# Attention and expert layer on one core: value products in three groups of four slots, and row-maximum units placed anew

## The chip, the cores and the metric

The kernel runs on one core of a Trainium2 chip. The metric is the device time of one execution in microseconds (us); lower is better. TensorE multiplies (PE in the rows; PEld is its weight load), VectorE is DVE, ScalarE is ACT, GpSimd is POOL, and SyncE (SP) issues most DMA transfers. The engines run their own instruction lists in order and meet at semaphores.

## The reference

One transformer layer on 8 batches of 1024 tokens of width 256: causal attention with 16 heads of 64, then a router over 32 experts with a capacity of 320 tokens.

```python
q_blhd = jnp.einsum('bld,dhk->blhk', x_bld, Wq)
latent_bll = jnp.einsum('bld,dc->blc', x_bld, Wkv_down)
k_blhd = jnp.einsum('blc,chk->blhk', latent_bll, Wk_up)
v_blhd = jnp.einsum('blc,chk->blhk', latent_bll, Wv_up)
attn = softmax(where(mask, q @ k / sqrt(64), neg_inf))
y_blhd = jnp.einsum('bhqk,bkhd->bqhd', attn, v_blhd)
x = _layernorm(x + jnp.einsum('bqhd,hdo->bqo', y_blhd, Wout))
x = _layernorm(x + _L0_ffn_ref(x, w_router, w_gate, w_up, w_down))
```

## The kernel before

Key and value projections are folded, so that scores are products of a projected query with a latent of 64 columns, and the value product multiplies probabilities with the latent itself (`lat_keys`). The outer loop runs over 64 **pairs** of heads (`gp`; `b` is the batch and `p` = 0 to 7 the pair in it). Each pair has 12 **slots** `t`: slots 0 to 3 are the first 512 queries against key tiles 0 to 3, slots 4 to 11 the second 512 queries against key tiles 0 to 7. Slots 0 to 3 and 8 to 11 lie on the diagonal and shrink (512, 384, 256, 128 queries); the other four have 512.

For a slot TensorE writes turned scores, keys on partitions, into one of three banks (`turned_scores`, L742 and L745; the two that shrink most hold both heads in one bank); ScalarE takes the exponential into one of NPROBS probability buffers (L1011); GpSimd zeroes the masked half of a diagonal block (`keep_past`, L491) and adds the buffers up (`add_probs`, L511 and L516); TensorE multiplies them with the latent (`values`, L765), the two heads side by side on 64 output columns each. Two slots make a group of value products, six groups in a pair. A buffer is free when its value product and its addition are done.

The softmax needs each query's maximum a pair ahead. 24 **units** for each pair (`row_scores`, L717, two to a place of PLACES) write untransposed scores into three more banks (`row_ps0`, `row_ps1`, half of `turned_ps1`), and VectorE takes a maximum from each (`row_max`, L1175 with a mask, L1179 without). A unit waits until the unit that had its bank three before is reduced. In PLACES, (t, 0) is after the scores of slot t and (t, 1) after what else the slot does. The places of a pair are numbered 0 to 11 below, in order. VectorE combines the maxima (L1183) and TensorE transposes them ("maxT", `turn_max`, L727, 8 columns), twice a pair, in slots 0 and 6.

LATE is a hand-written list of work by slot that shares one bank, `misc_ps`: the query projection of a later pair ("q", L664; ScalarE writes its high halves at L991 and L992, VectorE then its low halves at L1155 and L1156, and only then is the bank free), maxT, the sums ("sums", L777, inverted by VectorE at L1196 and spread by `invert_rows` at L1209 and L1213 in slots 6 and 8), and, in some pairs, the output projection ("proj", L787), transposes of x ("xT") and of its normalised sum ("x1T"), latents ("lat"), keys and the router. "proj" stands in pairs p = 0 and 1 of a batch, x1T in p = 2, xT and lat in p = 6, keys in p = 7. After the 64 pairs come the experts, which the change leaves in their order.

VectorE walks the same list: in a slot first the maxima of the units at (t, 0), then the low halves of a query from slot t-1, then the rest of LATE, `invert_rows`, and the units at (t, 1).

## Time and profile before

| | |
|---|---|
| median of 3 runs | 2441.88 us (2440.73 to 2442.39) |
| the profiled execution's own time | 2441.89 us |
| its span, first to last instruction | 2440.1 us |
| PE busy | 2319.8 us, 95% |
| POOL busy | 1715.3 us, 70% |
| DVE busy | 1517.1 us, 62% |
| ACT busy | 1041.7 us, 43% |
| mean granted TensorE clock | 0.974 |

Busy time is a union over an engine's instructions. TensorE's ends are modelled, so starts are what is read: the distance from one matmul's start to the next is what the first one costs. The three windows of 27.00 us from 147.20 on hold one pair each (p = 3, 4, 5 of batch 0), and repeat to within 0.02 us in TensorE's busy time; they stand for the pairs without extra work.

### The profile page before, as it was taken

The numbers are of one execution on the slowest core, as the hardware profiler recorded it, in microseconds if no ns is written. First come the engines' busy times: TensorE is split into PE (matmuls) and PEld (weight loads), VectorE is DVE, ScalarE is ACT, GpSimd is POOL, SyncE is SP. The second block draws the span as 40 slices with busy tenths as digits, with TensorE's granted clock in tenths as the row PEclk, the third lists the DMA queues.
The fourth block names the chain that finished last, engine by engine and source line by source line (L and its number), as shares of the span: only waits on it lengthen the run. The fifth ranks groups of instructions, "written<-read, shape, count | busy, mean of one in ns | idle before, by whom it ended". The sixth has DMA issues, their size and how long they took to land.

```text
span 2440.1 us, 36843 instructions
## 1 busy us (share of the span) xinstructions
PE 2319.8 (95%) x11528; PEld 1509.0 (62%) x11528; DVE 1517.1 (62%) x4450; ACT 1041.7 (43%) x2048; POOL 1715.3 (70%) x1774
## 2 busy tenths in 40 slices
PE   6999999999999999999999999999999999849996
PEld 5565576556655666567655765566656665537774
DVE  4677656765576657765776567656766577225553
ACT  3454435543455445443544354534554454112222
POOL 0688767986788667975797669867886679524444
PEclk8999999999999999999999999999999999969998
DMA  3222200200011001100020002100110011234552
GB/s 89 62 65 62 62 10 19 65 24 18 14 44 49 14 14 36 53 19 14 19 73 21 10 19 61 27 18 14 44 49 14 14 33 41 67 110 150 183 184 67
DMA packets 96819, 118.97 MB, mean 49 GB/s; under 512 B 12288, under 2 KB 75782, under 8 KB 96624
## 3 DMA queue, kind: packets, MB, share of 16 engines
q1 hardware_dynamic: 89712, 99.98, 14.9%
...
q8 instruction: 93, 1.52, 0.3%
...
## 4 chain that ended last, share of the span: by engine, by line
PE 83%; DVE 7%; issue 4%; POOL 3%; ACT 2%; DMA 0%; SPq 0%; DVEq 0%; POOLq 0%; ACTq 0%
PE value_ps L765 20%; PE misc_ps L787 9%; PE turned_ps L742 9%; PE turned_ps L745 9%; PE misc_ps L664 8%; PE row_ps L717 7%; PE turned_ps L938 6%; PE turned_ps L717 3%; PE misc_ps L777 2%; DVE rinv L1209 1%; PE value_ps L957 1%; PE misc_ps L957 1%; POOL half_sums L516 1%; DVE masked_row L1175 1%; PE misc_ps L813 1%
## 5 line engine op out<-in xcount | busy, mean ns | idle before, releaser
L1011 ACT ACTIVATE probs<-turned_ps 128x512 f32<-128x512 f32 (+2 forms) x1280 | 647.7, 555 | 779.6 <-PE turned_ps L745 749.1
L516 POOL TENSOR_TENSOR half_sums<-half_sums,probs 128x1024 f32<-128x1024 f32 (+3 forms) x512 | 832.2, 1625 | 30.0 <-ACT probs L1011 14.1
L765 PE MATMUL value_ps<-probs,lat_keys 128*64 128x512 f32 (+3 forms) x3072 | 589.1, 505 | 2.2 <-POOL probs L491 2.2
L742 PE MATMUL turned_ps<-q_hl,lat_hi 128*128 128x512 f32 (+2 forms) x1280 | 500.2, 393 | 1.5 <-ACT fold_v L1064 1.5
L745 PE MATMUL turned_ps<-q_max,lat_lo 65*128 65x512 f32 (+2 forms) x1280 | 480.4, 375 | 1.8 <-DMA q_max<-both_rows 1.8
L491 POOL TENSOR_SCALAR_AFFINE_SELECT probs<-probs 128x256 f32<-128x256 f32 x512 | 210.6, 411 | 354.6 <-ACT probs L1011 352.0
L1175 DVE CUSTOM_DVE_ANT_0 masked_row<-row_ps,future 128x512 bf16<-128x512 f32 (+4 forms) x707 | 344.7, 508 | 136.5 <-PE row_ps L717 130.4
L765 PEld LDWEIGHTS value_ps<-probs,lat_keys 128*64 128x64 f32 x3072 | 188.2, 137 | 278.0 <-issue 211.6
L511 POOL TENSOR_TENSOR half_sums<-probs 128x768 f32<-128x768 f32 (+1 forms) x128 | 269.6, 2106 | 118.7 <-ACT probs L1011 118.6
L717 PE MATMUL row_ps<-lat_hi,q_hl 128*128 128x512 f32 (+4 forms) x1026 | 340.6, 373 | 4.9 <-DVE neg_max L1175 4.0
L717 PEld LDWEIGHTS row_ps<-lat_hi,q_hl 128*128 128x128 f32 x1026 | 189.6, 191 | 150.7 <-issue 69.7
L742 PEld LDWEIGHTS turned_ps<-q_hl,lat_hi 128*128 128x128 f32 x1280 | 243.3, 190 | 39.2 <-ACT probs L1011 10.0
L745 PEld LDWEIGHTS turned_ps<-q_max,lat_lo 65*128 65x128 f32 x1280 | 244.2, 191 | 27.7 <-DMA q_max<-both_rows 2.3
L1179 DVE TENSOR_REDUCE unit_max<-row_ps 128x1 f32<-128x512 f32 (+1 forms) x319 | 199.9, 643 | 77.0 <-PE row_ps L717 77.0
L787 PE MATMUL misc_ps<-fold_v,headsT 128*128 128x256 f32 x1008 | 232.5, 383 | 6.3 <-DVE x L1237 3.6
L787 PEld LDWEIGHTS misc_ps<-fold_v,headsT 128*128 128x128 f32 x1008 | 187.6, 190 | 47.4 <-issue 13.9
L717 PE MATMUL turned_ps<-lat_hi,q_hl 128*128 128x320 f32 x510 | 182.4, 358 | 6.5 <-DVE unit_max L1175 2.7
L523 POOL TENSOR_TENSOR headsT<-headsT,rinv_rows 128x512 f32<-128x512 f32 x128 | 165.4, 1292 | 22.7 <-DVE rinv_rows L1213 22.7
L991 ACT CAST q_hl<-misc_ps 64x512 fp32r<-64x512 f32 x125 | 72.6, 581 | 216.6 <-PE misc_ps L664 216.6
L1175 DVE CUSTOM_DVE_ANT_0 masked_row<-turned_ps,future 128x256 bf16<-128x256 f32 (+1 forms) x317 | 160.6, 507 | 3.4 <-PE turned_ps L717 1.5
L938 PE MATMUL turned_ps<-ex_xT,ex_w 128*128 128x320 f32 x512 | 145.6, 438 | 0.0
L1237 DVE TENSOR_TENSOR x<-misc_ps,x_in 128x256 f32<-128x256 f32 x64 | 27.2, 425 | 186.7 <-PE misc_ps L787 186.7
...
## 6 DMA issues: line engine op xcount, KB each, us to landing
q_max<-q_hl SPq DMA_DIRECT2D x256, 128.0 KB
...
```

Of the source, the lines that this page charges most:

```text
L491: nc.gpsimd.affine_select(out=block, in_=block, pattern=[[0, 2], [1, P]], compare_op=ALU.is_ge, fill=0.0, base=0, channel_multiplier=-1).t ...
L511: nc.gpsimd.tensor_tensor(sums_of(gp, c)[:, :, q0:BANK], before[:, :, q0:BANK], now[:, :, q0:BANK], ALU.add).then_inc(added, 1)
L516: nc.gpsimd.tensor_tensor(total, total, now[:, :, q0:BANK], ALU.add).then_inc(added, 1)
L717: nc.tensor.matmul(dst[:, 0:k1 - k0], q_hl[gp % 2][:, h, i * P:(i + 1) * P], lat_hi[b % 2][:, k0:k1], start=True, stop=True).then_inc(rows ...
L742: nc.tensor.matmul(scores_of(n, h), lat_hi[b % 2][:, keys], q_hl[gp % 2][:, heads, cols], start=True, stop=False)
L745: nc.tensor.matmul(scores_of(n, h), lat_lo[b % 2][:, keys], q_max[:, c, heads, q0:BANK], start=False, stop=True).then_inc(turned_full, 1)
L765: mm = nc.tensor.matmul(value_ps[h * LD:(h + 1) * LD, q0:BANK], lat_keys[b % 2][:, j, :], probs[:, n % NPROBS, h, q0:BANK], start=(j == 0) ...
L787: mm = nc.tensor.matmul(bank[:, 0:D], headsT[:, (NPAIR * b + j) % NHEADS, i * P:(i + 1) * P], fold_v[:, j, :], start=(j == 0), stop=(j == ...
L938: mm = nc.tensor.matmul(turned_ps[f][:, m, 0:C], ex_w[e % AHEAD][:, m, kd, f * P:(f + 1) * P], ex_xT[:, g % 2, kd, u * C:(u + 1) * C], sta ...
L1011: nc.scalar.activation(probs[:, n % NPROBS, heads, q0:BANK], scores_of(n, h), ACT.Exp).then_inc(exp_done, 1)
L1175: nc.vector.tensor_tensor_reduce(masked_row[n % 2][:, 0:width], row[:, 0:width], future[:, BANK - width:], scale=-1.0, scalar=-MASKED, op0 ...
L1179: nc.vector.tensor_reduce(dst, row[:, 0:width], AX.X, ALU.max, negate=True).then_inc(max_done, 1)
```

## The change

Value products go in groups of four slots: slots 8 to 11 of the pair before in slot 1, slots 0 to 3 in slot 5, slots 4 to 7 in slot 9, each two slots behind its scores. There are eight probability buffers instead of six. The room comes from x: one buffer instead of two, and x is loaded a second time, straight into `x1`, where the output projection is added to it in place. The 12 places of the units, the sums (slot 4 to 5) and some LATE work (slot 5 to 4) move. `NOUT` only names a 2.

```diff
-    PLACES = [(0, 0), (0, 1), (1, 1), (2, 1), (4, 0), (4, 1), (6, 0), (7, 0), (8, 0), (8, 1), (10, 0), (10, 1)]
+    PLACES = [(0, 0), (1, 0), (1, 1), (3, 1), (4, 1), (5, 0), (5, 1), (7, 0), (8, 1), (9, 0), (9, 1), (10, 1)]
...
-    NPROBS = 6
-    VALUES = 2
+    NPROBS = 8
+    VALUES = 4
...
-        x_in = [sb(f"x_in{i}", [P, NT, D], F32, attn) for i in range(2)]
+        x_in = sb("x_in", [P, NT, D], F32, attn)
...
             if gp:
-                late[4].append(("sums", gp - 1))
+                late[5].append(("sums", gp - 1))
...
-                for i, t in enumerate((3, 5, 9, 10, 11)):
+                for i, t in enumerate((3, 4, 9, 10, 11)):
                     late[t].append(("proj", b - 1, 3 + i))
...
-                                  (3, 5, 7, 10)):
+                                  (3, 4, 7, 10)):
                     late[t].append(("x1T", b - 1, *use))
...
-                for t, c in zip((3, 5, 7, 8), (0, 2, 1, 3)):
+                for t, c in zip((3, 4, 7, 8), (0, 2, 1, 3)):
                     late[t].append(("xT", b + 1, c))
...
-                late[5].append(("keys", b + 1))
+                late[4].append(("keys", b + 1))
...
+                if p == NPAIR - 1:
+                    if b:
+                        sp.wait_ge(sent, 16 * NT * b)
+                    sp.dma_start(x1[:, :, 0:D], x_tiles[b]).then_inc(x1_loaded, 16)
...
-                    if t % VALUES == LAG % VALUES and gp * NSLOT + t >= VALUES + LAG:
-                        values(gp * NSLOT + t - LAG - VALUES)
+                    n0 = gp * NSLOT + t - LAG - (VALUES - 1)
+                    if n0 >= 0 and n0 % VALUES == 0:
+                        values(n0)
...
-                nc.vector.tensor_tensor(x1[:, i, 0:D], bank[:, 0:D], x_in[b % 2][:, i, :], ALU.add).then_inc(free_of(use), 1)
+                nc.vector.tensor_tensor(x1[:, i, 0:D], bank[:, 0:D], x1[:, i, 0:D], ALU.add).then_inc(free_of(use), 1)
```

Place A, TensorE of an ordinary pair before, from the projection "q" of slot 1 (its last row) to the second unit of place 4 (`row_ps0`, 128x320). L717 are units, L742 and L745 turned scores, L765 value products.

```order
L664 MATMUL misc_ps<-xT_lo,fold_hi 128x512 x2
L717 MATMUL row_ps1<-lat_hi0,q_hl1 128x384
L717 MATMUL turned_ps1<-lat_hi0,q_hl1 128x384
...
L765 MATMUL value_ps<-probs,lat_keys0 64x256 x2
L765 MATMUL value_ps<-probs,lat_keys0 64x128 x2
L717 MATMUL row_ps0<-lat_hi0,q_hl1 128x512
L717 MATMUL row_ps1<-lat_hi0,q_hl1 128x512
...
L717 MATMUL turned_ps1<-lat_hi0,q_hl1 128x320
L717 MATMUL row_ps0<-lat_hi0,q_hl1 128x320
```

The same place in the changed kernel, where lines stand 5 or 6 higher (L722 units, L747 and L750 scores, L670 "q"):

```order
L670 MATMUL misc_ps<-xT_lo,fold_hi 128x512 x2
L722 MATMUL row_ps1<-lat_hi0,q_hl1 128x384
L722 MATMUL turned_ps1<-lat_hi0,q_hl1 128x384
L747 MATMUL turned_ps1<-q_hl0,lat_hi0 128x512
...
L747 MATMUL turned_ps0<-q_hl0,lat_hi0 128x256
...
L722 MATMUL row_ps0<-lat_hi0,q_hl1 128x512
L722 MATMUL row_ps1<-lat_hi0,q_hl1 128x512
...
L722 MATMUL turned_ps1<-lat_hi0,q_hl1 128x320
L722 MATMUL row_ps0<-lat_hi0,q_hl1 128x320
```

The value group between the two uses of `row_ps0` is gone (it now stands ahead of "q").

Place B, VectorE between the two halves of the inversion in an ordinary pair. Before:

```order
L1175 ISA masked_row0,unit_max<-turned_ps1,future 128x256
...
L1175 ISA masked_row1,unit_max<-row_ps0,future 128x256
...
L1179 TENSOR_REDUCE unit_max<-row_ps1 128x1
L1179 TENSOR_REDUCE unit_max<-turned_ps1 128x1
L1209 RECIPROCAL rinv<-sums_cols 32x16 x4
L1213 STREAM_TRANSPOSE rinv_rows1<-rinv 128x512
```

And in the changed kernel (its lines 6 higher):

```order
L1181 ISA masked_row0,unit_max<-turned_ps1,future 128x256
...
L1181 ISA masked_row1,unit_max<-row_ps0,future 128x256
...
L1215 RECIPROCAL rinv<-sums_cols 32x16 x4
L1219 STREAM_TRANSPOSE rinv_rows1<-rinv 128x512
L1185 TENSOR_REDUCE unit_max<-row_ps1 128x1
L1185 TENSOR_REDUCE unit_max<-turned_ps1 128x1
```

The two maxima of place 8 now stand behind the second half of the inversion.

Place C, TensorE of the changed kernel from the value group of slot 9 to maxT of slot 0 in the next pair (L770 value products, L732 maxT):

```order
L770 MATMUL value_ps<-probs,lat_keys0 64x512 x8
L722 MATMUL turned_ps1<-lat_hi0,q_hl1 128x512
L722 MATMUL row_ps0<-lat_hi0,q_hl1 128x512
...
L722 MATMUL row_ps1<-lat_hi0,q_hl1 128x512
L722 MATMUL turned_ps1<-lat_hi0,q_hl1 128x512
...
L722 MATMUL row_ps0<-lat_hi0,q_hl0 128x128
L722 MATMUL row_ps1<-lat_hi0,q_hl0 128x128
L732 MATMUL misc_ps<-ident,neg_max1 8x128
```

Before, one place of units instead of two came between the last value group and slot 11, and another value group stood between the 128x128 units and maxT.

## Rows read from the trace of the kernel before

**Rows 1.** The page, part 1: busy time, share and instructions of TensorE.
```profile
PE 2319.8 (95%) x11528; PEld 1509.0 (62%) x11528; DVE 1517.1 (62%) x4450; ACT 1041.7 (43%) x2048; POOL 1715.3 (70%) x1774
```

**Rows 2.** Busy us of each engine in one ordinary pair, clock, DMA, GB/s.
```profile
147.20:174.20 27.00, 26.85 (x136) 16.13 (x137) 19.58 (x59) 13.43 (x28) 22.81 (x22) 1.00 0.24 70
```

**Rows 3.** Timeline of TensorE, that pair: start us, us, engine, line, tile.
```profile
152.08 0.87 PE L765 MATMUL value_ps<-probs,lat_keys 128*64 128x256 f32 x8
152.88 0.50 PE L717 MATMUL row_ps<-lat_hi,q_hl 128*128 128x512 f32 x1
...
161.50 0.27 PE L727 MATMUL misc_ps<-ident,neg_max 128*8 128x128 f32 x1
...
161.84 0.39 PE L745 MATMUL turned_ps<-q_max,lat_lo 65*128 65x512 f32 x1
...
169.59 0.40 PE L717 MATMUL turned_ps<-lat_hi,q_hl 128*128 128x512 f32 x1
169.83 0.40 PE L717 MATMUL row_ps<-lat_hi,q_hl 128*128 128x512 f32 x1
170.16 1.94 PE L765 MATMUL value_ps<-probs,lat_keys 128*64 128x512 f32 x8
172.03 0.50 PE L717 MATMUL row_ps<-lat_hi,q_hl 128*128 128x512 f32 x1
172.36 0.39 PE L717 MATMUL turned_ps<-lat_hi,q_hl 128*128 128x512 f32 x1
```

**Rows 4.** Timeline, all engines, from the end of slot 1's "q".
```profile
151.17 0.34 PE L717 MATMUL row_ps<-lat_hi,q_hl 128*128 128x384 f32 x1
...
153.32 0.69 DVE L1156 TENSOR_TENSOR q_hl<-misc_ps,q_hl 64x512 fp32r<-64x512 f32 x1
...
154.04 0.69 DVE L1175 CUSTOM_DVE_ANT_0 masked_row<-row_ps,future 128x512 bf16<-128x512 f32 x1
...
154.66 0.08 DVE L1175 DVE_READ_ACCUMULATOR2_ANT neg_max<- 128x1 f32 x1
...
154.79 0.19 PEld L717 LDWEIGHTS row_ps<-lat_hi,q_hl 128*128 128x128 f32 x1 [0.19 <-DVE neg_max L1175]
```

**Rows 5.** Timeline from the inversion on VectorE, and TensorE's stop at 163.73.
```profile
157.79 0.41 PE L717 MATMUL row_ps<-lat_hi,q_hl 128*128 128x320 f32 x1
...
157.93 0.72 DVE L1196 STREAM_TRANSPOSE sums_cols<-misc_ps 128x512 f32<-128x512 f32 x1 [1.77 <-PE misc_ps L777]
...
160.58 1.29 DVE L1179 TENSOR_REDUCE unit_max<-row_ps 128x1 f32<-128x512 f32 x2 [1.13 <-PE row_ps L717]
161.88 0.28 DVE L1190 CAST both_rows<-misc_ps 8x128 fp32r<-8x128 f32 x1
...
163.81 0.39 DVE L1175 CUSTOM_DVE_ANT_0 masked_row<-turned_ps,future 128x256 bf16<-128x256 f32 x1
...
164.48 0.69 DVE L1179 TENSOR_REDUCE unit_max<-row_ps 128x1 f32<-128x512 f32 x1
...
163.73 0.39 PE L717 MATMUL row_ps<-lat_hi,q_hl 128*128 128x512 f32 x1
164.27 0.50 PE L717 MATMUL turned_ps<-lat_hi,q_hl 128*128 128x512 f32 x1
```

**Rows 6.** Timeline of VectorE, last units of the pair and the combination.
```profile
172.56 0.69 DVE L1175 CUSTOM_DVE_ANT_0 masked_row<-row_ps,future 128x512 bf16<-128x512 f32 x1 [0.33 <-PE row_ps L717]
...
173.18 0.69 DVE L1175 CUSTOM_DVE_ANT_0 masked_row<-turned_ps,future 128x512 bf16<-128x512 f32 x1
...
173.91 0.17 DVE L1183 TENSOR_REDUCE neg_max<-unit_max 128x8 f32<-128x16 f32 x1
```

**Rows 7.** Timeline of TensorE in a pair p = 6: xT of slot 3, and "q" of slot 9.
```profile
1011.64 0.34 PE L717 MATMUL row_ps<-lat_hi,q_hl 128*128 128x384 f32 x1
...
1014.54 0.66 PE L674 MATMUL misc_ps<-ident,x_in 128*128 128x128 f32 x4 [0.20 <-DVE q_hl L1156]
...
1030.39 0.70 PE L664 MATMUL misc_ps<-xT_hi,fold_hi 128*128 128x512 f32 x2 [0.45 <-DVE xT_lo L1132]
```

More of the change, by code:

```diff
@@ L201, in build_layer @@
         end_free = [sem(f"end_free{i}") for i in range(3)]
-        x_loaded = [sem(f"x_loaded{i}") for i in range(2)]
+        x_loaded = sem("x_loaded")
+        x1_loaded = sem("x1_loaded")
         wkv_split = sem("wkv_split")
@@ L407, in _ @@
                     sp.wait_ge(alone_ready, b)
-                    sp.dma_start(out_tiles[b - 1], x_in[(b - 1) % 2][:, :, :]).then_inc(alone_stored, 16)
-                if b and p == 5 and b + 1 < B:
-                    sp.wait_ge(alone_stored, 16 * b)
-                    sp.dma_start(x_in[(b + 1) % 2][:, :, :], x_tiles[b + 1]).then_inc(x_loaded[(b + 1) % 2], 16)
+                    sp.dma_start(out_tiles[b - 1], x_in[:, :, :]).then_inc(alone_stored, 16)
+                if p == 5 and b + 1 < B:
+                    if b:
+                        sp.wait_ge(alone_stored, 16 * b)
+                    sp.dma_start(x_in[:, :, :], x_tiles[b + 1]).then_inc(x_loaded, 16)
             def load_weights(e):
@@ L432, in _ @@
             sp.wait_ge(alone_ready, B)
-            sp.dma_start(out_tiles[LAST], x_in[LAST % 2][:, :, :]).then_inc(alone_stored, 16)
+            sp.dma_start(out_tiles[LAST], x_in[:, :, :]).then_inc(alone_stored, 16)
             sp.wait_ge(sent, 16 * NT * B)
@@ L447, in _ @@
                 g = (e - AHEAD) // 2
-                sp.wait_ge(ex_sent[g % 2], 16 * NY * (g // 2 + 1))
+                sp.wait_ge(ex_sent[g % NOUT], 16 * NY * (g // NOUT + 1))
                 load_rows(e)
                 load_weights(e)
-            for k in range(2):
-                sp.wait_ge(ex_sent[k], 16 * NY * (E // 4))
+            for k in range(NOUT):
+                sp.wait_ge(ex_sent[k], 16 * NY * (E // 2 // NOUT))
         @block.gpsimd
@@ L671, in turn_x @@
                 kd, t0 = c // 2, HPB * (c % 2)
-                pe.wait_ge(x_loaded[b % 2], 16 * (b // 2 + 1))
+                pe.wait_ge(x_loaded, 16 * (b + 1))
                 for k in range(HPB):
-                    mm = nc.tensor.transpose(bank[:, k * P:(k + 1) * P], x_in[b % 2][:, t0 + k, kd * P:(kd + 1) * P],
-                                             ident[:, :])
+                    mm = nc.tensor.transpose(bank[:, k * P:(k + 1) * P], x_in[:, t0 + k, kd * P:(kd + 1) * P], ident[:, :])
                 mm.then_inc(full_of(use), 1)
@@ L902, in _ @@
                         row_scores(*unit)
-            for n0 in range(PAIRS * NSLOT - VALUES - LAG, PAIRS * NSLOT, VALUES):
-                values(n0)
+            values(PAIRS * NSLOT - VALUES)
             for use in ENDING:
@@ L1029, in pass_alone @@
             def pass_alone(b, i):
+                x_out = x_in
                 act.wait_ge(x1_ready, b * 2 + i // HPB + 1)
                 act.wait_ge(alone_scale, b * 2 + i // HPB + 1)
-                ins = nc.scalar.activation(x_in[b % 2][:, i, :], x1[:, i, 0:D], ACT.Identity, scale=alone[:, 2, i:i + 1])
+                ins = nc.scalar.activation(x_out[:, i, :], x1[:, i, 0:D], ACT.Identity, scale=alone[:, 2, i:i + 1])
                 if i == NT - 1:
```

24 lines of the change are left out of this document (11 added, 13 removed).

## The prediction

> **What bounds the kernel now.** I read the page first: TensorE is busy for 95% of the span, no other engine for more than 70% [rows 1]. Then windows of one pair: of 27.00 us in an ordinary pair TensorE is busy for 26.85 at a granted clock of 1.00 (the 2.4 GHz level), GpSimd for 22.81, VectorE for 19.58, ScalarE for 13.43 [rows 2]. So while the pairs run, what a matmul costs from its start to the next one's start is what counts, and the others matter only where TensorE stops for them. The timeline shows two kinds of loss, which busy time hides.
>
> The first is the change between value products and the rest. Ordinary neighbours of 512 columns start 0.24 us apart (169.59 to 169.83). From the last of them to the value group it is 0.33, and after the group, between 172.03 and 172.36, again 0.33 [rows 3]: 0.09 going in, 0.10 coming out. Inside, a group with 1024 columns for each head takes 170.16 to 172.03, 1.87 us, and one with 384 columns takes 152.08 to 152.88, 0.80. The line through both has 1.07 / 640 = 1.67 ns a column and 0.16 us that don't depend on columns. A group of value products thus costs about **0.35 us** beside its columns, whatever its length.
>
> The second is waits for a unit's bank. There are three banks, so TensorE can be only three units ahead of VectorE's maxima. Place A (slots 1 to 4): "q" ends and the first unit of place 2 starts at 151.17; VectorE then takes that place's maxima and the two low halves (second one at 153.32), starts the first maximum of place 3 at 154.04, and has it at 154.66 + 0.08. TensorE loads for the second unit of place 4, which needs this bank, at 154.79 [rows 4]. That is 3.62 us after "q", and it was waited for by only 0.11. Place B: the second unit of place 8 started 0.54 after the first, 163.73 to 164.27, 0.30 more than ordinary [rows 5]. With some 0.1 behind it and 0.1 for an exponential in slot 5, estimates from the same timeline, an ordinary pair has some 0.6 us of waits.
>
> **What the change saves.** Six groups become three: 3 x 0.35 = 1.05 us a pair. The columns stay.
>
> **What moving maxT costs.** Both maxT (8 columns of weights) stood behind a value group: there maxT and the first score after it take 161.50 to 161.84, 0.34 [rows 3], where without maxT the first matmul takes 0.33. It was free. Now both stand alone. At least 0.10 each (only the first score after it is longer), at most 0.35 each (a full change). I take 0.2, nearer to the entry and exit of 0.19 that the value group shows without its 0.16 inside.
>
> Of this the page "TensorEngine Tiling (Array Packing)" of the Trainium skill, section Key Properties, says that changing the tiling mode drains TensorE. By this rule a maxT alone is a change of its own, and only one of three changes a pair is really saved, 0.35 instead of 0.65 net. The trace agrees for value groups (the 0.35 above) and doesn't show a maxT alone at full clock.
>
> **What the new order costs.** VectorE's list is nearly the same as before (the order shows it), with the same times per instruction. So I walk TensorE against it, from three moments at which VectorE is idle or its place is known. Units and scores cost 0.235 us per 512 columns (0.175 for 384, 0.15 for 320, 0.12 for 256), "q" six times 512, 1.40.
>
> *Place A.* From the end of "q": units 0.35, scores of slots 2 and 3 0.71, place 3 0.47, scores of slot 4 0.94, first unit of place 4 0.15: TensorE is at its second unit after 2.62. It needs the bank of the first unit of place 3, and VectorE's chain to there is unchanged, 3.62 [rows 4]. Before, the value group of 0.80 and its 0.19 stood in between. Wait: **1.00**.
>
> *Place B.* From the first unit of place 6, right behind the sums. VectorE starts the inversion 0.14 later (157.93 against 157.79, where TensorE's next matmul starts) and goes on: inversion 0.72 (less an overlap of some 0.08), maxima of place 6 1.30 (160.58 to 161.88), the maxT copy and the first half of `invert_rows` 1.93 (to 163.81), place 7 0.67 (to 164.48) [rows 5], the second half of `invert_rows` 1.75 (as the first, without the copy), first maximum of place 8 0.69: 7.1, release 7.2. TensorE: place 6 0.57, slot 6 0.94, maxT 0.15, slot 7 0.94, place 7 0.24, slot 8 0.94 with 0.11 of waiting for an exponential, "q" 1.40, place 8 0.47, slot 9 0.70, first unit of place 9 0.18: 6.64. The second unit of place 9 needs that bank. Wait **0.6**, and the 0.11. The maxT here is hidden in it.
>
> *Place C.* From the first unit of place 10, behind the value group of slot 9. VectorE starts 0.53 later (172.03 to 172.56 before), two maxima 1.29, then two masked ones and the combination, 172.56 to 173.91 + 0.17, 1.52 [rows 5, 6]: 3.34. TensorE: place 10 0.57, slot 10 0.47, place 11 0.47, slot 11 0.24, slot 0 0.94, place 0 0.12: 2.81, then maxT, which waits for the combination. A value group used to cover this. Wait: **0.53**, and the 0.2 of maxT behind it.
>
> Ordinary pair: -1.05 + 0.2 + 1.00 + 0.71 + 0.53 - 0.6 = **+0.8 us**.
>
> The other pairs, by the same walk:
> - p = 0: "q" is in slot 7, and its low halves stand ahead of the second half of `invert_rows`. "q" ends 4.24 after the sums; low halves from 1.45 after it, 1.42 for both [rows 4]; 1.75; 0.69: 9.55 against 6.53. Wait 3.0 at place 9 instead of 0.6. The projections of slots 9 to 11 cover place C. -1.05 + 0.2 + 1.00 + 3.06 - 0.2 = +3.0.
> - p = 1: the same at B, and at slot 3 "proj" needs `misc_ps`, free 2.90 after "q" ended (1011.64 to 1014.54, and there TensorE came early, by 0.20 in idle time and some 0.35 in starts [rows 7]). Now it comes at 1.06: wait 1.84 instead of A's 1.00, with 0.35 of waits before. +3.7.
> - p = 2: 1.84 at x1T of slot 3, then x1T cover B and C. +0.3.
> - p = 6: 1.84 at xT of slot 3, and two xT each wait for ScalarE's and VectorE's halves of the one before: 2.75 at A for 0.35, 3.9 at B (xT of slots 7 and 8 ahead of `invert_rows`) for 0.6 (one of 0.45 + 0.15 shown at 1030.39 [rows 7]), 1.0 more at C, where the value group no longer stands ahead of "lat". +5.9. This is the roughest one.
> - p = 7: the copy of the keys comes ahead of place 4. +1.1.
>
> Sum: 27 ordinary pairs 22, p = 0 seven times 21, p = 1 26, p = 2 2, p = 6 seven times 41, p = 7 8: **+120 us** on the profiled execution's 2441.89, which is the median of the runs (2441.88) too. 2562, said as **2560**.
>
> **Costed at nothing.** Second load of x (8 x 1 MB): issued on SP in p = 7 ahead of the next query's transfers, which SP issues after slot 3 and TensorE needs a third of a pair later; `add_x` comes nine slots after. Should it delay that query row by its transfer, each batch pays at most a few us. Waiting for `sent` there stops SP with only that behind it; sending ends a pair earlier. Reading x in place of `x_in` is the same addition. The eight buffers end ScalarE's waits for old value products; TensorE waited for ScalarE by 0.1 a pair. GpSimd: the addition of slot 5 waits for the sums, which read its buffer, now later; from there its 14.3 us to the last diagonal block (22.81 [rows 2] less what lies behind) end 2 us before the value group of slot 1 needs it. The experts are unchanged.
>
> **Rivals.**
> - *The saving decides.* If VectorE gives back those banks early enough, the pair loses 1.05 and pays 0.2: -0.85 x 64 = -54, **2388**. For it: VectorE is idle for 27% of the pair [rows 2]. Against it: at the three places its chain is without idle time in the rows. It decides as soon as the three waits together stay under 1.45 (0.85 + the old 0.6); I have 2.24. Chance 0.12.
> - *Only the ordinary waits.* +0.8 in all pairs, the extra waits of p = 0, 1, 6 lying in each other's shadow: +51, **2493**. Against: each starts from a place where VectorE had caught up. Chance 0.2.
> - *GpSimd too.* In p = 5 and 6 it also sends four tiles, and the value group of slot 5 needs slot 3's mask with 1.3 us to spare. If that is used up, 2 to 3 us in 14 pairs: +35, **2595**. Chance 0.1.
> - *maxT as a full change*, by its upper bound of 0.35 (the section cited above would have it so): +0.15 on most pairs, **2570**. Chance 0.05.
> - *No change of cost*, groups of four paying inside what two groups paid and the waits as long as before: **2442**. Chance 0.03.
>
> **How the numbers follow.** My forecast holds 0.5, by itself 2530 to 2590. To leave out no more than 2 in 10, the range takes in the second and third rival: 2480 to 2600. About 0.2% (5 us) is what a measurement of this kernel can tell from no change. Faster 0.12, same 0.03, slower 0.85.
>
> **What the profile after would show.** Ordinary pairs of 27.8 us instead of 27.0; value groups 192 instead of 384, sixteen records each, with 0.16 + 1.67 ns a column. TensorE idle or late at the second unit of place 4 (3.6 after "q"), the second of place 9, and at maxT of slot 0, all released by VectorE; pairs p = 0, 1 and 6 longer by 3 to 6 us; the stretch of the experts as long as before. I am wrong if ordinary pairs come out under 27.0, which means one of the three chains is shorter than in the rows of before, or if the lost time lies with GpSimd or with the transfer of x.

## The result, and the profile after

The changed kernel takes **2656.42 us** (median of 4 runs, 2655.98 to 2657.02), before 2441.31 us beside it. The ratio is 1.088 (95% interval 1.086 to 1.090): 215 us slower, where the prediction said 120, and 56 us beyond the end of its range. The profiled execution's span is 2655.3 us.

Part 1 of the page of the changed kernel, and the first line of part 4, the chain that ended last:

```profile
PE 2392.5 (90%) x11528; PEld 1573.3 (59%) x11528; DVE 1501.8 (57%) x4450; ACT 1026.0 (39%) x2048; POOL 1713.8 (65%) x1774
...
PE 68%; DVE 18%; issue 9%; ACT 3%; POOL 1%; DMA 0%; DVEq 0%; SPq 0%; POOLq 0%; ACTq 0%
```

Of VectorE the page of before had 7% in that chain; it is 18% now. And TensorE is *busy for longer* than in [rows 1], 2392.5 us against 2319.8, with the same 11528 matmuls and fewer group changes. That can't be a wait. The mean granted clock points to the reason: 0.946 against 0.974. The trace has only two values of it, 1.00 and 0.50, so that is 2 x 0.054 x 2655 = 287 us at half clock (1.2 GHz) against 2 x 0.026 x 2440 = 127 before.

Windows of one pair each in the changed kernel: an ordinary one (p = 3 of batch 0), then p = 1, 2, 3 and 6 of batch 2. Columns: start and end, us, busy us of TensorE, its weight load, VectorE, ScalarE, GpSimd, granted clock, DMA share, GB/s.

```profile
148.47:176.52 28.05, 26.99 (x136) 16.45 (x135) 19.33 (x59) 13.10 (x27) 22.79 (x22) 1.00 0.24 67
636.06:687.33 51.27, 46.88 (x216) 33.49 (x215) 23.19 (x73) 14.78 (x30) 26.09 (x29) 0.93 0.05 11
687.33:723.25 35.92, 33.07 (x184) 23.10 (x183) 20.93 (x66) 17.67 (x36) 26.10 (x29) 0.95 0.07 16
723.25:755.71 32.46, 30.79 (x145) 18.30 (x144) 22.93 (x67) 16.75 (x35) 19.92 (x19) 0.89 0.04 9
811.64:856.88 45.24, 36.44 (x164) 23.06 (x163) 23.12 (x66) 17.45 (x35) 30.09 (x28) 0.89 0.12 30
```

The last four in the kernel before, in the same order:

```profile
585.77:629.99 44.22, 44.02 (x216) 31.50 (x215) 23.58 (x73) 15.08 (x30) 26.15 (x29) 1.00 0.06 13
629.99:664.15 34.16, 33.57 (x183) 22.72 (x182) 21.55 (x67) 17.74 (x35) 26.11 (x29) 0.96 0.08 17
664.15:693.55 29.40, 29.38 (x145) 17.30 (x145) 22.58 (x66) 16.78 (x36) 20.00 (x19) 0.94 0.04 10
747.52:782.50 34.98, 32.19 (x166) 20.44 (x164) 22.88 (x66) 17.57 (x34) 31.05 (x30) 1.00 0.15 39
```

The ordinary pair is 28.05 us at full clock, 27.8 predicted. Four of the other pairs run in part at half clock. Over batches 1 to 6 this is 6.8 us of each p = 1, 3.4 of p = 2, 6.8 of p = 3 and 10.2 of p = 6. Before, it was 0.7 us of p = 2, 2.7 of p = 3 and none of the others. VectorE's work in a pair grew by 0.35 us at most.

TensorE's timeline in the ordinary pair: maxT of slot 0, place A, maxT of slot 6, place B, the value group of slot 9.

```profile
148.65 0.34 PE L722 MATMUL row_ps<-lat_hi,q_hl 128*128 128x128 f32 x2
149.38 0.27 PE L732 MATMUL misc_ps<-ident,neg_max 128*8 128x128 f32 x1 [0.39 <-DVE neg_max L1189]
...
154.32 0.34 PE L722 MATMUL row_ps<-lat_hi,q_hl 128*128 128x384 f32 x1
...
157.22 0.42 PE L722 MATMUL turned_ps<-lat_hi,q_hl 128*128 128x320 f32 x1
157.95 0.41 PE L722 MATMUL row_ps<-lat_hi,q_hl 128*128 128x320 f32 x1 [0.31 <-DVE neg_max L1181]
...
164.33 0.27 PE L732 MATMUL misc_ps<-ident,neg_max 128*8 128x128 f32 x1
164.36 0.48 PE L747 MATMUL turned_ps<-q_hl,lat_hi 128*128 128x512 f32 x1
164.68 0.40 PE L750 MATMUL turned_ps<-q_max,lat_lo 65*128 65x512 f32 x1
...
169.38 0.33 PE L722 MATMUL row_ps<-lat_hi,q_hl 128*128 128x384 f32 x1
169.94 0.45 PE L722 MATMUL row_ps<-lat_hi,q_hl 128*128 128x384 f32 x1 [0.23 <-DVE unit_max L1185]
170.31 3.65 PE L770 MATMUL value_ps<-probs,lat_keys 128*64 128x512 f32 x16
173.90 0.50 PE L722 MATMUL turned_ps<-lat_hi,q_hl 128*128 128x512 f32 x1
```

All three places wait for VectorE. The second unit of place 4 starts 3.63 us after "q" ended (157.95 - 154.32; predicted 3.62, against [rows 4]). The value group takes 3.59 (predicted 0.16 + 2048 x 1.67 ns = 3.58). A maxT alone at full clock costs 0.03 (164.33 to 164.36) and lengthens the score behind it from 0.24 to 0.32: 0.11, about the predicted lower bound of 0.10.

Two of the new long waits, in p = 1 of batch 2: "proj" of slot 3, and the second unit of place 9.

```profile
644.26 0.48 PE L792 MATMUL misc_ps<-fold_v,headsT 128*128 128x256 f32 x1 [1.68 <-DVE q_hl L1162]
...
665.95 0.34 PE L722 MATMUL row_ps<-lat_hi,q_hl 128*128 128x384 f32 x1
668.87 0.69 PE L722 MATMUL row_ps<-lat_hi,q_hl 128*128 128x384 f32 x1 [2.59 <-DVE unit_max L1185]
```

And short windows there, for each of the two the wait and what follows it:

```profile
641.30:644.70 3.40, 1.72 (x9) 1.36 (x9) 2.42 (x6) 2.53 (x5) 1.27 (x2) 1.00 0.26 58
644.80:648.10 3.30, 3.30 (x9) 2.64 (x8) 0.00 (x0) 0.00 (x0) 3.12 (x4) 0.50 0.07 17
665.90:668.60 2.70, 0.38 (x3) 0.06 (x1) 2.51 (x7) 1.39 (x4) 2.21 (x8) 1.00 0.00 0
668.70:672.00 3.30, 3.13 (x7) 1.06 (x9) 1.67 (x6) 0.00 (x0) 3.30 (x3) 0.50 0.00 0
```

TensorE stood for 1.68 us and for 2.59 us; "proj" behind the first and the value products behind the second ran at a granted clock of 0.50.

In p = 3 it is different. Its 6.8 us at half clock start at 723.3 us, 0.9 us behind the logits of the router, 32 matmuls of 32 columns. TensorE had not stood there: it was busy for 6.09 of the 6.20 us up to 723.2. The logits and the window at half clock, in the changed kernel and then in the kernel before:

```profile
718.82 3.76 PE L818 MATMUL misc_ps<-wr,x1T 128*128 128x32 f32 x32
723.30:730.10 6.80, 6.35 (x21) 3.53 (x21) 4.04 (x15) 2.50 (x5) 3.34 (x5) 0.50 0.01 3
...
658.43 4.60 PE L813 MATMUL misc_ps<-wr,x1T 128*128 128x32 f32 x32
661.20:667.90 6.70, 6.70 (x23) 4.20 (x22) 3.47 (x11) 1.59 (x3) 3.07 (x4) 0.50 0.01 2
```

Half clock at this spot is not new. Before, it comes inside or right behind the logits in six of seven batches, mostly for half as long; in the changed kernel it comes in all seven.

### The profile page after: what moved, and what is told of

Its sections match the earlier page's. It is cut to its first block, busy times and chain, and to the rows that moved or that the text cites. A ratio compares the mean times of both kernels' runs of the same rounds, so it can differ in the third digit from the quotient of the medians.

```text
span 2655.3 us, 36721 instructions
## 1 busy us (share of the span) xinstructions
PE 2392.5 (90%) x11528; PEld 1573.3 (59%) x11528; DVE 1501.8 (57%) x4450; ACT 1026.0 (39%) x2048; POOL 1713.8 (65%) x1774
## 4 chain that ended last, share of the span: by engine, by line
PE 68%; DVE 18%; issue 9%; ACT 3%; POOL 1%; DMA 0%; DVEq 0%; SPq 0%; POOLq 0%; ACTq 0%
PE value_ps L770 21%; PE misc_ps L792 9%; PE misc_ps L670 7%; PE row_ps L722 6%; PE turned_ps L943 5%; PE turned_ps L747 4%; DVE unit_max L1185 4%; PE turned_ps L750 4%; DVE masked_row L1181 4%; DVE rinv L1215 3%; PE misc_ps L782 2%; PE turned_ps L722 2%; DVE q_hl L1162 2%; DVE q_hl L1161 1%; PE misc_ps L962 1%
## 5 line engine op out<-in xcount | busy, mean ns | idle before, releaser
L770 PE MATMUL value_ps<-probs,lat_keys 128*64 128x512 f32 (+3 forms) x3072 | 569.0, 514 | 0.0
L747 PE MATMUL turned_ps<-q_hl,lat_hi 128*128 128x512 f32 (+2 forms) x1280 | 512.0, 401 | 7.7 <-ACT probs L1016 3.2
L750 PE MATMUL turned_ps<-q_max,lat_lo 65*128 65x512 f32 (+2 forms) x1280 | 485.7, 382 | 0.9 <-DMA q_max<-both_rows 0.9
L722 PE MATMUL row_ps<-lat_hi,q_hl 128*128 128x512 f32 (+4 forms) x1026 | 352.7, 376 | 77.6 <-DVE unit_max L1185 60.9
L770 PEld LDWEIGHTS value_ps<-probs,lat_keys 128*64 128x64 f32 x3072 | 211.1, 142 | 305.4 <-issue 274.7
L747 PEld LDWEIGHTS turned_ps<-q_hl,lat_hi 128*128 128x128 f32 x1280 | 249.1, 195 | 94.9 <-ACT probs L1016 52.7
L722 PEld LDWEIGHTS row_ps<-lat_hi,q_hl 128*128 128x128 f32 x1026 | 191.2, 196 | 182.6 <-DVE unit_max L1185 79.2
L750 PEld LDWEIGHTS turned_ps<-q_max,lat_lo 65*128 65x128 f32 x1280 | 248.9, 194 | 31.6 <-DMA q_max<-both_rows 1.6
L792 PE MATMUL misc_ps<-fold_v,headsT 128*128 128x256 f32 x1008 | 244.3, 397 | 15.4 <-DVE q_hl L1162 11.7
L792 PEld LDWEIGHTS misc_ps<-fold_v,headsT 128*128 128x128 f32 x1008 | 195.9, 198 | 61.6 <-DVE q_hl L1162 13.2
L722 PE MATMUL turned_ps<-lat_hi,q_hl 128*128 128x320 f32 x510 | 194.2, 381 | 8.2 <-DVE unit_max L1185 4.8
L1185 DVE TENSOR_REDUCE unit_max<-turned_ps 128x1 f32<-128x512 f32 (+1 forms) x193 | 119.0, 617 | 128.5 <-PE turned_ps L722 113.8
L1241 DVE TENSOR_TENSOR x<-misc_ps,x 128x256 f32<-128x256 f32 x64 | 27.2, 425 | 253.2 <-PE misc_ps L792 253.2
```

The costliest lines, as they stand in the source:

```text
L722: nc.tensor.matmul(dst[:, 0:k1 - k0], q_hl[gp % 2][:, h, i * P:(i + 1) * P], lat_hi[b % 2][:, k0:k1], start=True, stop=True).then_inc(rows ...
L747: nc.tensor.matmul(scores_of(n, h), lat_hi[b % 2][:, keys], q_hl[gp % 2][:, heads, cols], start=True, stop=False)
L750: nc.tensor.matmul(scores_of(n, h), lat_lo[b % 2][:, keys], q_max[:, c, heads, q0:BANK], start=False, stop=True).then_inc(turned_full, 1)
L770: mm = nc.tensor.matmul(value_ps[h * LD:(h + 1) * LD, q0:BANK], lat_keys[b % 2][:, j, :], probs[:, n % NPROBS, h, q0:BANK], start=(j == 0) ...
L792: mm = nc.tensor.matmul(bank[:, 0:D], headsT[:, (NPAIR * b + j) % NHEADS, i * P:(i + 1) * P], fold_v[:, j, :], start=(j == 0), stop=(j == ...
L1185: nc.vector.tensor_reduce(dst, row[:, 0:width], AX.X, ALU.max, negate=True).then_inc(max_done, 1)
```

## The experiments

The theory after the result: the value groups that were taken out had covered waits for VectorE's chain, as predicted, and some of the longer new waits bring TensorE's clock to 1.2 GHz, which the prediction didn't have. Rivals: the buffers and the second load of x, the places of the units by themselves, and a clock that has nothing to do with the waits. All kernels compute the reference in full; two add matmuls whose result is overwritten.

A table of the pairs serves all of them: us from a pair's first exponential to the next pair's, means over batches 1 to 6. The second row is before plus the prediction's terms. The runs e4, e5, e7, e8, e9 and e13 are told with the pairs that moved.

| kernel | p=0 | 1 | 2 | 3 | 4, 5 | 6 | 7 | whole |
|---|---|---|---|---|---|---|---|---|
| before | 37.1 | 44.2 | 33.1 | 29.0 | 27.0 | 35.0 | 27.3 | 2441 |
| predicted | 40.1 | 47.9 | 33.4 | 29.8 | 27.8 | 40.9 | 28.4 | 2560 |
| changed | 40.9 | 51.3 | 35.9 | 32.5 | 28.0 | 45.2 | 28.4 | 2656 |
| e2_groups | 38.9 | 45.9 | 34.2 | 33.3 | 29.2 | 39.5 | 29.9 | 2595 |
| e3_places | 38.2 | 46.0 | 34.9 | 30.3 | 27.1 | 38.1 | 27.4 | 2509 |
| e6_fill | 40.9 | 48.1 | 34.3 | 30.9 | 28.0 | 41.9 | 28.4 | 2597 |
| e10_combo | 38.6 | 46.2 | 34.4 | 32.7 | 27.4 | 39.9 | 27.8 | 2541 |
| e12_early_q | 38.1 | 46.3 | 34.1 | 31.8 | 26.9, 27.5 | 40.8 | 27.9 | 2536 |

**The buffers alone.** The kernel before with NPROBS = 8, one x and the load into x1; VALUES = 2 and every place as before.

```diff
-    NPROBS = 6
+    NPROBS = 8
...
+                    sp.dma_start(x1[:, :, 0:D], x_tiles[b]).then_inc(x1_loaded, 16)
```

> Before, with the buffers of the change alone: eight probability buffers, one buffer of x, x loaded a second time into x1 and added in place; groups of two, old places. My theory (the groups uncover VectorE's chain, and the clock falls behind the long waits) expects no difference: 2441 us, 2435 to 2446. The rival that the second load, the in-place addition or the single buffer costs something expects over 2450, and up to 2656 if it were all of it.

Measured: 2441.66 us, ratio 1.000 (0.999 to 1.001). The second load, the addition in place and the two buffers cost and bring nothing.

**The groups without the places.** The changed kernel with the old PLACES and the old LATE slots.

```diff
-    PLACES = [(0, 0), (1, 0), (1, 1), (3, 1), (4, 1), (5, 0), (5, 1), (7, 0), (8, 1), (9, 0), (9, 1), (10, 1)]
+    PLACES = [(0, 0), (0, 1), (1, 1), (2, 1), (4, 0), (4, 1), (6, 0), (7, 0), (8, 0), (8, 1), (10, 0), (10, 1)]
```

> The changed kernel with the places of the units, the sums and the slot-5 work where they were before: only the grouping and the buffers are changed. My theory puts the loss on the value groups that no longer stand between TensorE and VectorE's maxima, so the old places should not save it: over 2560 us, about 2620. The rival that the new places are what costs expects less than 2480, and by the saving of the groups alone 2390.

**The places without the groups.** The opposite edit, in the kernel before.

> Before, with the new places of units, sums and slot-5 work, but groups of two in their old slots. By my theory a value group still stands ahead of place 4 and behind place 11, and slot 3's work still comes too early for no one: 2441 to 2500 us, 2465 by half of the waits at place B. The rival that the places alone are the loss expects over 2560 us.

Measured: e2 2595.26 us, ratio 1.063 (1.062 to 1.065); e3 2508.85 us, 1.026 (1.024 to 1.028). Alone the groups cost 153 us and the places 67; together 215. So most of it is the grouping, and e2 is inside what was expected. The expectation for e3 was too low (at most 2500): the places cost nothing in an ordinary pair (27.1) but 1 to 3 us in p = 0 to 3 and 6. With groups of four the new places gain 1.2 us in the ordinary pair (29.2 to 28.0), 1.5 in p = 7 and 0.8 in p = 3, but lose 2.0, 5.4, 1.7 and 5.7 in p = 0, 1, 2 and 6: 61 us more in all, with 287 us at half clock instead of 154. The ordinary pair of e2:

```profile
152.66:181.86 29.20, 27.13 (x136) 16.35 (x135) 19.32 (x59) 13.24 (x26) 22.86 (x22) 1.00 0.22 64
```

TensorE is busy in it for 27.13 us, in the changed kernel's for 26.99: of the 1.15 us between the two pairs, 1.0 is time in which TensorE waits.

**The clock.** Idle matmuls in front of the long waits, nothing moved.

```diff
+            def fill(gp, t, count):
+                m = scored(gp * NSLOT + t)
+                pe.wait_ge(exp_done, m - 2)
+                for _ in range(count):
+                    nc.tensor.matmul(SCORE_BANKS[m % 3], lat_hi[gp // NPAIR % 2][:, 0:P], q_hl[gp % 2][:, 0, BANK:2 * BANK],
+                                     start=True, stop=True)
...
+                        if b and p in (0, 1, 6) and unit[1] == 19:
+                            fill(gp, t, 9)
...
+                    if b and p in (1, 2, 6) and t == 3 and gp < PAIRS - 2:
+                        fill(gp, t, 6)
```

> The changed kernel with idle matmuls of 512 columns (their result is overwritten by the next scores) put where TensorE waits longest: six ahead of slot 3's work in p = 1, 2 and 6, nine ahead of the second unit of place 9 in p = 0, 1 and 6, from batch 1 on. They take 1.4 and 2.1 us, less than the waits of 1.83 and 2.7 us, so the waits' ends stay. If the low clock behind these waits is what costs the unpredicted part, the stretches at half clock in p = 1, p = 2 and the first of p = 6 go: 8.5 us a batch, 2656 - 60 = 2596 us (2580 to 2615). If the clock has nothing to do with the waits, or costs nothing, 2656 us (2650 to 2665).

Measured: **2596.50 us**, ratio 1.064 (1.062 to 1.065), mean clock 0.976. More work, 60 us less time. The same wait of p = 1 in its timeline (L899 is the fill), then the windows of its pairs p = 1, 2, 3 and 6 of batch 2:

```profile
654.02 0.34 PE L722 MATMUL row_ps<-lat_hi,q_hl 128*128 128x384 f32 x1
654.19 2.25 PE L899 MATMUL turned_ps<-q_hl,lat_hi 128*128 128x512 f32 x9
656.94 0.44 PE L722 MATMUL row_ps<-lat_hi,q_hl 128*128 128x384 f32 x1 [0.50 <-DVE unit_max L1197]
```

```profile
625.78:673.88 48.10, 47.16 (x231) 34.57 (x230) 23.18 (x73) 14.79 (x29) 26.11 (x29) 1.00 0.05 12
673.88:708.23 34.35, 32.90 (x190) 22.91 (x189) 20.93 (x66) 17.44 (x36) 26.10 (x29) 1.00 0.08 17
708.23:738.86 30.63, 27.84 (x145) 16.83 (x144) 22.92 (x67) 16.43 (x35) 20.00 (x19) 1.00 0.04 10
794.78:836.48 41.70, 35.75 (x181) 23.51 (x179) 23.11 (x66) 17.33 (x35) 30.11 (x28) 1.00 0.13 33
```

The second unit of place 9 starts 2.92 us after the first, as in the changed kernel (665.95 to 668.87): the wait is as long, only filled. The clock is 1.00 in all four windows, and the whole kernel has 2 x 0.024 x 2593 = 124 us at half clock, no more than before's 127. Since nothing but the fill was added, what TensorE does in the filled waits is shown to decide the clock behind them, and the half clock that the change added to cost some 60 us.

Two things limit this reading. p = 3 gained without a fill of its own (32.5 to 30.9 us in the table): half clock behind its logits came in two of seven batches instead of seven, and the run doesn't show why. And the length of a wait doesn't decide alone. In p = 6 the wait for "lat" at slot 10 was not filled. It lasted 2.2 us in both kernels. The changed kernel has 6.8 us at half clock behind it in each of batches 1 to 6, e6 has 3.4 us in one of them. The changed kernel's wait of 2.58 us at place 9 of p = 0 is followed by full clock in all seven batches.

**Place B.** VectorE's second half of the inversion later, in slot 11.

```diff
-                    if gp and t in (6, 8):
+                    late_half = 8 if gp == PAIRS - 1 else 11
+                    if gp and t in (6, late_half):
```

> The changed kernel with VectorE's second half of the inversion (L1215, L1219 for c = 1) in slot 11 instead of slot 8, behind the maxima of place 11. If place B waits for these 1.75 us, as predicted, the second unit of place 9 no longer waits: 0.4 less in the ordinary pair (28.0 to 27.6), 2.7 less in p = 0 and p = 1, 2.6 in p = 6, and the half clock behind it goes in p = 1 and p = 6 (1.7 and 5.1 us): 14 + 7 x (8.0 + 6.8) = 118 less, 2540 us (2520 to 2580). If VectorE's list as a whole is too long there, the wait returns at the combination or at the projection of slot 1: over 2620.

Measured: 2653.68 us, ratio 1.088 (1.086 to 1.091): 3 us less, no gain to speak of; the rival's number held. Timeline of p = 4 in batch 0, TensorE and then VectorE:

```profile
178.78 0.28 PE L722 MATMUL turned_ps<-lat_hi,q_hl 128*128 128x256 f32 x1
179.92 0.38 PE L722 MATMUL row_ps<-lat_hi,q_hl 128*128 128x256 f32 x1 [0.86 <-DVE neg_max L1181]
...
177.85 1.07 DVE L1215 RECIPROCAL rinv<-sums_cols 32x16 f32<-32x16 f32 x4
178.96 0.71 DVE L1219 STREAM_TRANSPOSE rinv_rows<-rinv 128x512 f32<-128x512 f32 x1
179.60 0.25 DVE L1181 CUSTOM_DVE_ANT_0 masked_row<-row_ps,future 128x128 bf16<-128x128 f32 x1
```

In the ordinary pair place 9 no longer waits (0.7 us of 2.6 are left in p = 0 and 1), but the inversion now stands in front of place 0's maxima, and the second unit of place 1 waits for these by 0.86. The same edit with slot 9 instead of 11 puts it beside the value group:

> The changed kernel with VectorE's second half of the inversion in slot 9, behind the maxima of place 9 and the low halves, in front of place 10. TensorE then has the value group of slot 9 to do, 3.59 us, so these 1.75 us should be covered on both sides: the ordinary pair 28.0 to 27.6 us, p = 0, 1 and 6 by 1.75 us each, with the half clock behind place 9 in p = 1 and p = 6 (1.7 to 5 us): 14 + 7 x (5.2 + 3.5) = 75 less, 2580 us (2560 to 2610). If the wait only moves on to place C, as it moved on to place 1 with the inversion in slot 11: 2640 to 2660.

Measured: **2570.91 us**, ratio 1.052 (1.045 to 1.058): 86 us less by one line that moves 1.75 us of VectorE's work to where TensorE has 3.59 us of its own. The wait at place 9 of p = 0 falls from 2.57 to 0.72 us, by about the 1.75 that were moved; the ordinary pair goes from 28.0 to 27.7, and the time at half clock from 287 to 191 us. Place B is shown, and that the cover decides, not the amount of work.

**Slot 3.** `late[t].insert(0, ...)` in slots 4 and 5 for proj, x1T and xT, instead of `append` in 3 and 4.

> The changed kernel with the misc_ps work of slots 3 and 4 (proj in p = 1, x1T in p = 2, xT in p = 6) in slots 4 and 5, ahead of the sums. If slot 3's wait of 1.83 us for VectorE's low halves is a wait of its own, it goes with the half clock behind it: (1.8 + 1.7) x 3 pairs x 7 batches = 73 less, 2583 us (2560 to 2610). If it only stands for the wait at place A, which would come in its place (1.0 us each), 2656 - 7 x 3 x (0.8 + 1.7) = 2604 or, with the clock still falling behind it, 2640.

Measured: 2645.16 us, ratio 1.083 (1.081 to 1.085), 11 less: neither of the two, nearest to "the clock still falls". p = 2 became 1.9 us shorter (35.9 to 34.0), but p = 1 only 0.9: its wait at slot 3 is gone, that at place 9 stays. And p = 0, which the edit doesn't touch, became longer (40.9 to 42.2): half clock now follows its wait at place 9, 2.58 us as before, in four of seven batches.

**Place C.** maxT behind the scores of slot 1.

```diff
-            late[0 if gp else HPB - 1].append(("maxT", gp, 1))
+            if gp:
+                EARLY[gp, 1] = [("maxT", gp, 1)]
+            else:
+                late[HPB - 1].append(("maxT", gp, 1))
```

> The changed kernel with the maxT of slot 0 moved behind the scores of slot 1, ahead of place 1 and the value group. If place C is a wait for VectorE's combination (0.58 us in the trace), 0.7 us more of work in front covers it: 0.5 less in all pairs but p = 0 and 1, 2656 - 25 = 2631 us (2622 to 2640). If the wait is VectorE's lateness as such, it moves to the projection of slot 1, which needs the bank that maxT's copy frees: 2656 us (2650 to 2660).

Measured: 2631.19 us, ratio 1.079 (1.077 to 1.080): 25 less, the number expected, and 27.5 in the ordinary pair, 0.5 less (in p = 4 and 5 of batches 1 to 6 0.4 and 0.3): place C is a wait of its own. In p = 1, whose work in slot 11 had covered place C, nothing was gained. But that the whole agrees is partly luck. In batches 1 to 6 p = 6 became 2.8 us shorter and p = 2 1.3, with 6.8 and 2.9 us less at half clock, and p = 0 2.2 us longer, with 6.3 us more of it, though its wait at place 9 is 2.58 us as before. The moves of the half clock are as large as what was tested.

**Place A.** (5, 0) instead of (4, 1) in PLACES.

> The changed kernel with the two units of place 4 moved from slot 4 to slot 5, behind its scores. If place A is a wait for the bank of the first unit of place 3, 0.94 us more of work in front covers the 0.73 us that the trace shows: 0.7 less in 50 pairs, 2656 - 35 = 2621 us (2610 to 2635). If the maxima of places 4 and 5 then come too late for place 6 or for the inversion, the wait moves there: 2656 us or more.

Measured: 2673.62 us, ratio 1.095 (1.093 to 1.097): 17 more. Timeline of its ordinary pair, place 4 and place 5:

```profile
159.17 0.63 PE L724 MATMUL row_ps<-lat_hi,q_hl 128*128 128x320 f32 x2
159.98 0.41 PE L724 MATMUL turned_ps<-lat_hi,q_hl 128*128 128x320 f32 x1 [0.18 <-DVE unit_max L1187]
```

The first row holds the second unit of place 4 and the first of place 5, the last row the second of place 5. Place 4 doesn't wait; place 5, whose second unit is now the fourth in a row on three banks, does. The ordinary pair stays at 28.0, so the wait moved, as the rival had it. Most of the 17 us come from elsewhere: 1.8 us in each p = 0, which has 4.0 us at half clock where it had none.

**The moves together.** maxT of slot 0, slot 3's work, the inversion in slot 9.

> The three moves together: maxT of slot 0 behind the scores of slot 1, slot 3's and 4's work in slots 4 and 5, the second half of the inversion in slot 9. If the three waits are separate, their gains add: 2656 - 25 - 11 - 75 = 2545 us (2500 to 2570), ordinary pair 27.1 us (28.0 - 0.5 - 0.4). If they are one shortage of VectorE's time, the moves share one gain: about 2580, as the inversion's move alone.

Measured: 2541.08 us, ratio 1.040 (1.033 to 1.046): 115 less than the changed kernel, 122 by the single runs. The whole adds, and so does the ordinary pair (0.6 less, beside 0.3 and 0.4 by the single runs). Pair by pair it doesn't: p = 0 became 2.3 us shorter where the single runs sum to 1.5 longer, p = 6 5.3 shorter where they sum to 7.7, since each run has its half clock in other places. Against one shared gain (2580) the measurement is clear.

The same kernel with a fill:

> The three moves together, and idle matmuls again, fewer: two ahead of slot 4's work in p = 1, 2 and 6, four ahead of the second unit of place 9 in p = 0, 1 and 6. If shorter waits no longer pull the clock down, the fill gains nothing and costs up to 0.3 us a pair: 0 to 8 us over the three moves alone. If the clock still falls there, it gains 3.4 us of half clock and more each: 20 to 40 us less than the three moves alone.

Measured: 2552.86 us, ratio 1.044 (1.037 to 1.051), 12 more than without the fill. It gained nothing, and cost a little more than the 0 to 8 us expected. Time at half clock rose from 160 to 184 us, most of it in p = 6 (2.1 to 4.7 us, and the pair from 39.9 to 40.9), so this fill doesn't tell what still brings the clock down in p = 2, 3 and 6.

And the three moves with the projection of slot 1 earlier:

> The three moves together, and in the pairs without work in slot 11 before them the projection of slot 1 in slot 0, with maxT behind the value group of slot 1. VectorE's low halves (1.42 us) then come two places earlier and no longer stand in the chain to place 4. If place A is this chain, the ordinary pair loses 0.7 us more (27.1 to 26.4, under the 27.0 of before), p = 0 and 6 too: 35 us less than the three moves alone, and near or under before. If VectorE has no time to spare there, the wait comes back at place 4 or at a place ahead of it: the ordinary pair stays at 27.1.

Measured: 2535.95 us, ratio 1.037 (1.031 to 1.044). Windows of its ordinary pair and of p = 6 in batch 2, and TensorE's timeline where the ordinary pair waits now:

```profile
145.94:172.78 26.84, 26.23 (x136) 16.38 (x135) 19.32 (x59) 13.21 (x26) 22.80 (x22) 1.00 0.24 70
773.48:814.46 40.98, 33.98 (x163) 22.03 (x162) 23.00 (x66) 17.36 (x35) 30.25 (x28) 0.93 0.13 33
```

```profile
153.59 0.50 PE L756 MATMUL turned_ps<-q_max,lat_lo 65*128 65x512 f32 x1 [0.48 <-DMA q_max<-both_rows]
```

The wait at place 4 is gone with the low halves out of its chain, so it was that chain. Of the 0.7 us 0.5 are gained; the later maxT brings its transfer 0.48 too late. With 26.84 us this pair is now shorter than before's 27.00, by 0.16 of the 0.85 us that the prediction's first rival had for it; TensorE is busy in it for 0.62 us less than before. In batches 1 to 6 p = 4 has 26.9 but p = 5 27.5. The whole gains 5 us of the 35 expected, as p = 6 gets longer (39.9 to 40.8, with 4.2 us at half clock instead of 2.1).

**What is left in p = 6.**

```diff
-                late[9 if p == NPAIR - 2 else 7 if b and p < 2 else 8].append(("q", gp + 2, 0))
+                late[7 if b and p < 2 else 8].append(("q", gp + 2, 0))
...
-                for t, c in zip((4, 5, 7, 8), (0, 2, 1, 3)):
+                for t, c in zip((2, 4, 5, 7), (0, 2, 1, 3)):
...
-                late[10].append(("lat", b + 1, 0))
+                late[9].append(("lat", b + 1, 0))
```

> The kernel of e12_early_q with the work of p = 6 placed anew: xT in slots 2, 4, 5 and 7 instead of 4, 5, 7 and 8, the projection in slot 8 instead of 9, the first latents in slot 9 instead of 10. In e12_early_q the latents of slot 10 wait 2.36 us for the bank that VectorE's low halves of slot 9's projection free, with 6.8 us at half clock behind it. If that chain is what is left of p = 6, the value group of slot 9 (3.6 us) now covers it, and the waits at xT of slots 5 and 8 shrink too: 2 to 5 us less in 7 pairs, 2536 - 25 = 2511 us (2500 to 2522), p = 6 from 40.8 to about 37. If p = 6 is bound by VectorE and ScalarE as a whole, the waits move to xT of slot 2 and to the last latents: 2530 to 2540 us.

Measured: 2529.32 us, ratio 1.036 (1.035 to 1.038), 7 less. TensorE's timeline in p = 6 at place 10, and VectorE's beside it:

```profile
803.35 0.79 PE L728 MATMUL turned_ps<-lat_hi,q_hl 128*128 128x512 f32 x1 [3.20 <-DVE unit_max L1191]
...
800.18 0.68 DVE L1153 TENSOR_TENSOR lat_lo<-misc_ps,lat_hi 64x512 fp32r<-64x512 f32 x1 [3.93 <-ACT x1T L997]
800.90 1.08 DVE L1221 RECIPROCAL rinv<-sums_cols 32x16 f32<-32x16 f32 x4
...
802.64 0.65 DVE L1191 TENSOR_REDUCE unit_max<-turned_ps 128x1 f32<-128x512 f32 x1
```

The wait for the first latents went, and one of 3.20 came at place 10: VectorE idles for 3.93 us until ScalarE has written the latents, and behind that it has the second half of the inversion before place 10's maxima. The number is the second theory's, but the mechanism is neither's: it is the order of VectorE's list, not its load, for it idles there.

And the kernel before with the same idea:

> Before, with the work of p = 6 packed closer: xT in slots 3, 5, 6 and 7 instead of 3, 5, 7 and 8, and the projection in slot 8 instead of 9, in front of a value group and ahead of the latents. If the chain from the projection to the latents is a wait in before too (0.60 + 0.89 us in the trace), it is covered: 1.0 to 1.5 us less in 7 pairs, 2441 - 8 = 2433 us (2430 to 2438). If VectorE is what is late there, the wait goes to xT or to the last latents: 2438 to 2448 us.

Measured: 2441.03 us, ratio 1.000 (0.999 to 1.001), p = 6 35.0 as before. In batch 2 the wait of 0.82 us at the first latents is gone, one of 0.52 came at an xT, and that of 1.32 at the last latents stayed.

None of the runs beats the kernel before.

## Why the prediction was wrong, by its own steps

**Right: the ordinary pair.** 27.8 predicted, 28.0 measured, p = 7 28.4 and 28.4. The value group's line (0.16 + 1.67 ns a column) held, and the three places were named rightly. VectorE's three deadlines held too. The second unit of place 4 starts 3.63 us after "q" (3.62 predicted), the second unit of place 9 7.11 after the first of place 6 (7.2), and maxT 3.52 after the first unit of place 10 (3.34). What was less right is when TensorE gets there, so that two of the three waits are shorter than forecast. With the ordinary 0.15, 0.18 and 0.12 taken off, they are 0.58 at A (1.00 predicted), 0.38 at B (0.6) and 0.61 at C (0.53). At A TensorE had lost 0.43 before it came there (2.90 us from the end of "q" to the first unit of place 4, 2.47 in the walk). So errors in the parts cancel in the number of the pair. maxT alone is 0.11, not 0.2, and not 0.35: it did not act as a change of its own, and the rival of the full change falls.

**Right: what was costed at nothing.** Second load, addition in place, buffers: 0 (e1). The value products waited for GpSimd by 0.0 us in the page of the changed kernel (2.2 before), and it has 1% of the chain in part 4 (3% before).

**Wrong: the sum was taken at full clock.** The missing term is the granted clock. The step that failed is "I walk TensorE against it", with column prices of the 2.4 GHz level throughout. The prediction found waits of 1.84, 3.0 and 3.9 us and priced each at its own length, and every matmul behind them at full clock. The waits are there: 1.68 us at slot 3, 2.6 at place 9 of p = 0 and 1, and in p = 6 0.96, 2.49 and 2.19 one after the other. What the runs showed in place of the step: behind those of p = 1, 2 and 6 the clock is 0.50, the time at half clock grows from 127 to 287 us, and filling the waits gives back 60 us (e6).

The page "TensorE: Matmul & The Clock Gate" of the Trainium skill, in its section Terms, prices throttled time at time x (1 - K/N), which at half rate is half of it. By that rule, as an estimate, the 160 us more at half clock are 80 us. The runs gave back 60, though no more time at half clock was left than before. In p = 1 and 2 the rule holds nearly: 3.2 of 6.8 us and 1.6 of 3.4. In p = 3 and 6 less comes back, 1.6 of 6.2 and 3.3 of 9.7 us, because TensorE, now faster, waits longer further on: in batch 2 for 1.56 us instead of 0.45 at place 1 of p = 3, and for 1.32 instead of 0.73 at the last latents of p = 6.

**Mis-sized: the waits of other pairs.** With the clock repaired (e6) the pairs show the waits nearly alone. p = 0: +3.8 us (3.0 predicted), p = 1 +3.9 (3.7), p = 6 +6.9 (5.9, "the roughest one"), but p = 2 +1.2 (0.3) and p = 3 +1.9 (0.8 as an ordinary pair). Of p = 3 the walk had left out the router. VectorE's timeline in the changed kernel, from the logits to place 0's maxima, and TensorE's second unit of place 1, there and in e6:

```profile
722.62 0.42 DVE L1272 COPY router<-misc_ps 128x256 f32<-128x256 f32 x1 [2.82 <-PE misc_ps L818]
...
725.92 0.28 DVE L1181 CUSTOM_DVE_ANT_0 masked_row<-row_ps,future 128x128 bf16<-128x128 f32 x1
...
726.26 0.58 PE L722 MATMUL row_ps<-lat_hi,q_hl 128*128 128x256 f32 x1 [0.45 <-DVE neg_max L1181]
...
711.24 0.39 PE L722 MATMUL row_ps<-lat_hi,q_hl 128*128 128x256 f32 x1 [1.56 <-DVE neg_max L1193]
```

VectorE is 3.3 us with the router before it takes place 0's maxima. Before, a value group stood between these and maxT, and TensorE's idle time in the whole of p = 3 of batch 2 was 0.02 us. At full clock the wait is 1.56 us, enough for the 1.1 us; that it is what they are was read from the traces and not tried. Beyond the prediction these are 0.8 + 0.2 + 0.9 + 1.1 + 1.0 and 0.2 in each of p = 4 and 5, some 4.4 us a batch or 31 us in seven: with the clock's 60, 91 of the 95 that were missing.

**The rivals.** "The saving decides" fell for this order. e12 shows that part of the saving is there once the three places are covered: 0.16 us of 0.85 in an ordinary pair (26.84). "Only the ordinary waits" fell, for p = 0, 1 and 6 have waits beyond the ordinary ones. "GpSimd too" fell: no value product waited for it, and p = 5, which sends tiles, takes 28.0 us, p = 4 27.9.

**Open.** e13 still has 88 us over before: p = 6 +4, p = 3 +3, p = 1 +2, with half clock in p = 2, 3 and 6. What brings that clock down was not told apart, since the smaller fill of e11 didn't take it away. Nor is it known when a wait does. In e8_place4 the wait of 2.58 us at place 9 of p = 1 is followed by half clock in five batches and by full clock in two. A run that fills only one kind of wait, or that changes only the logits ahead of p = 3, was not made.
